# Five answer buffers instead of three, and the landing waits moved from GpSimd to the sync engine, in a mixture-of-experts scatter loop

## What is computed

```python
logits = tokens @ router_w.T
probs = softmax(logits)
rw, re = top_k(probs, 2)                  # each token goes to 2 of 8 experts
rw = rw / rw.sum(-1)
out = tokens
for e in range(8):
    h = gelu(tokens @ w1[e] + b1[e])
    y = h @ w2[e] + b2[e]
    out = out + combine[:, e:e+1] * y     # combine holds rw
```

## Time and profile before

| what | value |
|---|---|
| median of 3 runs | 1566.51 us (1566.21 to 1567.62) |
| the profiled execution's own time | 1572.86 us |
| its span in the trace | 1571.2 us |
| granted TensorE clock, mean over the span | 0.929 |
| second loop, first scatter to last scatter | 892.2 to 1478.3 us |

### The profile page before, as it was taken

The page is one execution under the profiler, slowest core; times in us unless marked ns, Lnnn a source line. Parts: engine busy times, 40 slices in busy tenths (PEclk is TensorE's granted clock), DMA queues, the critical chain, the costliest instruction groups (busy, mean ns, idle before and its releaser), DMA issues. The chain is left out here.

```text
span 1571.2 us, 29272 instructions
## 1 busy us (share of the span) xinstructions
PE 1320.0 (84%) x8768; PEld 1153.5 (73%) x8768; DVE 1018.6 (65%) x3667; ACT 1034.2 (66%) x2256; POOL 919.6 (59%) x932
## 2 busy tenths in 40 slices
PE   2899999999999999999971888888888887887154
PEld 2788888888888888888851777777777777777144
DVE  5488888888887877877856555555555555555022
ACT  2678878878888878888652756666665766665022
POOL 3116556556565665665555167877878787878500
PEclk7999999999999999999975899999999999999567
DMA  8535354354532222321225567777778777776699
GB/s 268 181 115 157 103 165 144 115 166 130 156 108 93 89 99 82 109 99 49 76 82 176 167 117 119 136 128 135 122 128 137 129 135 119 137 128 71 107 408 389
DMA packets 140394, 218.86 MB, mean 139 GB/s; under 512 B 39504, under 2 KB 89936, under 8 KB 139984
## 3 DMA queue, kind: packets, MB, share of 16 engines
q1 hardware_dynamic: 78224, 126.74, 26.4%
q0 software_dynamic: 53184, 71.34, 25.7%
q10 hardware_dynamic: 8832, 18.91, 3.2%
HBM read 103.04 MB, written 118.15 MB: 141 GB/s over the span
## 5 line engine op out<-in xcount | busy, mean ns | idle before, releaser
L1645 POOL DMA_INDIRECT sums<-yy,dest_i x284 | 456.7, 1608 | 162.6 <-issue 68.6
L1509 POOL DMA_INDIRECT sent<-tn,slot_s x256 | 278.3, 1087 | 160.5 <-DVE slot_s L1331 84.6
L1694 PE MATMUL s_bank<-band,hh 128*128 x568 | 175.2, 309 | 91.3 <-DVE yy L1789 91.3
L1789 DVE TENSOR_TENSOR yy<-s_bank,b_all 128x512 f32<-128x512 f32 x142 | 91.5, 686 | 245.4 <-DMA sums<-yy,dest_i 245.2
L1735 ACT ACTIVATE hid<-m_bank,b1s 128x512 f32<-128x512 f32 x142 | 97.4, 688 | 172.5 <-PE m_bank L1677 157.8
L1694 PEld LDWEIGHTS s_bank<-band,hh 128*128 128x128 f32 x568 | 115.6, 204 | 105.4 <-issue 105.3
L1694 PE MATMUL s_bank<-w_s,hh 128*128 x568 | 167.8, 295 | 0.0
L1694 PE MATMUL s_bank<-band,hl 128*128 x568 | 167.7, 295 | 0.0
L1488 POOL TENSOR_TENSOR rs<-ve,halves 128x4 f32<-128x4 f32 x64 | 64.8, 1019 | 151.1 <-DVE ve L1176 151.1
L749 PE MATMUL m_bank<-wvo,band 128*128 128x258 f32 x792 | 133.2, 304 | 13.3 <-DVE band L1317 10.9
L781 PE MATMUL o_bank<-vv,at 128*128 128x256 f32 x512 | 139.8, 396 | 1.3 <-DVE tt L1227 0.7
(11 more groups left out here) (213 smaller groups left out, 3447.6 us busy)
## 6 DMA issues: line engine op xcount, KB each, us to landing
xin<-sent SPq DMA_DIRECT2D x71, 520.0 KB, 4.6
xs<-in_x SPq DMA_DIRECT2D x32, 512.0 KB, 5.0
raw<-in_x SPq DMA_DIRECT2D x32, 512.0 KB
sums<-tt SPq DMA_DIRECT2D x32, 512.0 KB, 3.2
got<-sums SPq DMA_DIRECT2D x32, 512.0 KB, 6.7
out_x<-fin ACTq DMA_DIRECT2D x32, 512.0 KB, 9.0
sums<-yy,dest_i POOLq DMA_INDIRECT x284
raw<-in_x SPq DMA_DIRECT2D x64, 64.0 KB
```

The source lines that it names most:

```text
L1509: eng.indirect_dma_start(sent, bass.IndirectOffsetOnAxis(slot_s[:, par, j, k:k + 1], 0), tn[:, par, k, :], None).then_inc(scattered[par], 16)
L1645: eng.indirect_dma_start(sums, bass.IndirectOffsetOnAxis(dest_i[:, at_ % RING, k:k + 1], 0), yy[:, slot, k, :], None, compute_op=ALU.add). ...
L1694: last = eng.matmul(y_bank[half][:, k * C:(k + 1) * C], hx[:, par, f, ts], rhs, start=(n == 0), stop=(n == 3 * CC - 1))
L1789: eng.tensor_tensor(yy[:, slot, 2 * half:2 * half + 2, :], y_bank[half][:, :].rearrange("p (k c) -> p k c", k=2), b2_all[:, bass.ds(e, 1), ...
```

## The change

The number of `yy` buffers goes from 3 to 5, and with it the number of `rows_out` semaphores and the number of first tiles (n = 1 to 5 in place of 1 to 3) whose wait for tile n-1 is unconditional. The waits for the landings of tiles n-2 and n-1 leave GpSimd. SP takes them in the same round, after its load, and then raises a new semaphore `others_in` by one; GpSimd waits for `others_in` to reach n. What must have landed before a tile's scatters begin stays the same for tiles from 6 on. VectorE waits for the landing of tile n-5 in place of n-3.

```diff
-        YB = 3
+        YB = 5
...
+        others_in = sem("others_in")
...
             @block.sync
...
+                    if it.runs("Z") and it.block("Z") > 0:
+                        at_ = it.block("Z")
+                        if at_ > 1:
+                            eng.wait_ge(rows_out[(at_ - 2) % YB], ((at_ - 2) // YB + 1) * 16 * KT)
+                        if at_ <= YB:
+                            eng.wait_ge(rows_out[(at_ - 1) % YB], 16 * KT)
+                        else:
+                            turn = eng.value_load(turn_i[0:1, at_ - 1:at_], min_val=16 * KT, max_val=16 * KT * TURNS)
+                            eng.wait_ge(rows_out[(at_ - 1) % YB], turn)
+                        eng.sem_inc(others_in, 1)
...
             @block.gpsimd
...
                         if at_ > 0:
-                            if at_ <= YB:
-                                eng.wait_ge(rows_out[(at_ - 1) % YB], 16 * KT)
-                            else:
-                                turn = eng.value_load(turn_i[0:1, at_ - 1:at_], min_val=16 * KT, max_val=16 * KT * TURNS)
-                                eng.wait_ge(rows_out[(at_ - 1) % YB], turn)
-                        if at_ > 1:
-                            eng.wait_ge(rows_out[(at_ - 2) % YB], ((at_ - 2) // YB + 1) * 16 * KT)
+                            eng.wait_ge(others_in, at_)
                         alone(eng, (scaled_d.sem, scaled_d.count(it.before(), "Ys")), (scaled_a.sem, scaled_a.count(it, "Zs")))
```

## The result

The change takes 1557.51 us (median of 4, 1555.85 to 1559.08) against 1567.07 us of the kernel before on the same chip: a ratio of 0.9937 with a 95% interval of 0.992 to 0.9955, or 9.6 us less.

A forecast was written before the change was run, and what follows sets the result against it. GpSimd was taken to bound the loop by its scatters and ten landing waits. Waits falling from 46.8 to 37.2 us took 1566.5 us down 9.6 us to 1557 us, range 1550 to 1569 us.

The forecast's parts named there:

- Parts 1 and 2: Second loop: two more buffers gain 0; tiles 4 and 5 each pay a full landing wait instead of 0.3 us.
- the sum: GpSimd's landing waits in the second loop: 46.8 us before, 37.2 us after, difference -9.6 us.
- Part 3: GpSimd learns of landings through SP and `others_in`: adds 0.1 us per landing wait, bounds 0 and 0.76 us.
- the quiet case: GpSimd's landing wait at the start, with a load issued 4.05 us before the last scatter's end: 2.88 us.
- Part 4: SP's loads, timed by landings, go out 3.8 us before a tile's end; all twelve landing waits become 3.1 us.
- The seven waits: GpSimd's landing waits at expert changes: 34.1 us before, 4.88 us each, predicted to become 3.1 us each.
- the thinnest cover: Front's lead over GpSimd two tiles behind an expert change: 14.9 against 18.3 us, leaving 3.4 us.
- Part 5: VectorE's two line 1777 instructions lengthen GpSimd scatters: 13 us now, taken as unchanged; bounds -13 and +24 us.
- The scatter that lost nothing: GpSimd scatter starting 0.54 us after VectorE's line 1777 work: 1.57 us, read as agreeing only in part with the port rule.
- the costly phase: Timing of VectorE's line 1777 work against scatter starts: claimed narrow; 0.54 us ahead cost nothing, 0.64 us cost 0.52 us.
- the chances: Whole kernel: faster 0.64, from 0.60 less a range tail and 0.03; slower 0.22; same 0.14.

The follow-up runs named there:

- The two load runs: Changed kernel with tiles loaded one round earlier and SP's load before its wait for tile n-1, with three or no further table reads: ratios 1.0072 and 0.9952.

## Why the prediction was right

**What bounds.** GpSimd's scatters and its waits for landings, and not the 245 us on VectorE. The run without first waits shows it most directly: 16 us fewer of GpSimd's waits made the kernel 16 us faster (25.6 against 9.6 us), with no new long wait on GpSimd.

**Parts 1 and 2, the buffers.** Worth 0, and two more first waits. Five against three buffers gave the same ratio once the first waits were gone, and seem to cost 4 us with them (0.9937 against 0.9911, with intervals that overlap); tiles 4 and 5 waited 3.05 and 4.58 us, 7.0 us over their ordinary gaps, where the sum had 5.6 us.

**Part 3, the detour.** The waits over SP came out at 2.98 to 3.14 us where nothing else stretched them, against 2.88 and 3.07 us in the quiet case of before. Counted from the landing's last DMA packet to the next scatter, it is 1.11 to 1.15 us in the kernel before and 1.15 to 1.23 us in the change (without the last expert change). So the hop is near or below the 0.1 us of the sum.

**Part 4, the loads.** This is where the gain came from. The loads fell 3.6 us before a tile's end in the median, where 3.8 us were worked out, and 4.2 us after the end of the tile before; at a change none was in flight. The seven waits fell by 12.3 us (34.1 to 21.8); the sum had 12.4 us. The two load runs on one chip confirm the cause. The front was early enough: every tile from 2 on was weighted 5.8 us or more before its first scatter, where the thinnest cover was worked out as 3.4 us.

**Part 5, the pair.** Taken as unchanged, it gave 3.0 us back in the profiled executions (456.7 to 453.7 us). It was the largest open term and the one that moves most from version to version: 449.1 to 459.5 us over the eleven that kept the pair. Three readings in the prediction do not hold. Not in every case was it the pair: of the 53 scatters over 1.62 us in the kernel before, ten met VectorE's weighting of `yy` (line 1795) and lost up to 0.14 us, that of 1.67 us at 1093.74 us in the earlier trace rows among them. The scatter that lost nothing was no exception, since it began 0.54 us into the instruction, near its end. And the costly phase is not narrow: with a scatter every 1.87 us, a pair costs something wherever one begins in some 1.1 us. By the losses measured above, which fall from 0.55 us to nothing within each of the two instructions, the mean over all phases is an estimated 2 x 0.55 x 0.55 / 2 / 1.87 = 0.16 us a tile, 11 us in 71 tiles, so that a term near its old 13 us was to be expected.

The sum of the waits was -9.6 us; the profiles show 39.3 us in place of 46.8 us, -7.5 us, and the pair's -3.0 us. So the median's -9.6 us agrees with the sum partly by luck, by two small errors of opposite sign. The error in the waits is in two of the first ones, at tile 2 (3.79 us) and tile 5 (4.58 us): I had taken every landing without a load in flight to be quiet. For tile 5 the last load ahead was issued 7 us before tile 4's end and the landing was stretched all the same; the same came back in one other profile (4.46 us in the run without the pair) and not in the runs with the load one round earlier (3.0 to 3.2 us). The trace's DMA packets show what was in flight. Besides the data, they have packets of 16 KB of the kind `instruction`, which the page of the changed kernel lists as one queue:

```profile
q8 instruction: 74, 1.21, 0.3%
```

A landing with no load in flight usually has its last packet 1.8 to 2.0 us after the scatter's end. Over all profiles nine came later, at 2.2 to 3.4 us: that of tile 1 (GpSimd's wait at tile 2) in seven, and that of tile 4 (its wait at tile 5) in the change and in the run without the pair. In all nine such a packet began 0.3 to 0.8 us after the scatter's end, and the landing's last packet came 0.72 to 0.77 us after this one had ended. Four such packets that ended by 1.2 us stretched nothing. So the fetching of the program's own instructions is the likely cause, but no run takes it away, and the prediction had no term for it.

One slip lies in the chances: 0.60 less a tail, plus 0.03, cannot be 0.64.

On the port rule of the Trainium skill ("SBUF — State Buffer", section "Who interferes with whom"): the run without the pair and the rows beside it agree that a VectorE instruction with two SBUF inputs holds up GpSimd's indirect DMAs, and more closely than the prediction's "only in part" had it. A scatter that began inside one waited for what was left of it less 0.13 us. What the rule does not give is the mean, because it hangs on the phase: 9.6 us over 71 tiles, 0.14 us a tile, where the prediction's reading of it had up to 0.64 us.

## What to carry to other kernels

When the engine that waits longest is waiting for another's landings, look at how long finished work lies in front of that other engine: here 7 to 17 us, and more buffers bought nothing. A change that seems to move only waits can retime transfers; ask what each engine issues behind the wait it was given. And where an ordering wait for a landing is on the path, it pays to keep large loads out of its last few microseconds.

## What the runs showed of the hardware

The landing of GpSimd's indirect adding DMA takes longer with a 520 KB load in flight. With a load issued up to 1.5 us before the last scatter's end, GpSimd stood still for 4.5 to 5.3 us at expert changes in four kernels (6.1 us at most, in the run with five further reads). With one issued 2.1 to 2.4 us before it was 3.9 to 4.6 us, with one 2.8 to 3.8 us before 3.0 to 4.4 us, and with none in flight 2.9 to 3.1 us (in most profiles with five buffers 3.5 us at the last change).

A VectorE `tensor_tensor` of 128x512 with both inputs in SBUF lengthens an indirect DMA on GpSimd that begins while it runs, by what is left of the VectorE instruction less 0.13 us, up to 0.52 us. The mean over all 284 starts was 0.03 us. With one input in PSUM it did nothing.

The kernel before took 1567, 1568, 1573 and 1627 us in four sessions. In the slowest, nearly all of the additional time seems to lie ahead of the loop studied here; the kernel before has no trace there, but the version with the load 3.8 us before the end has one in both of the last two sessions. In the slowest its scatters were at:

```profile
L1650 POOL DMA_INDIRECT sums<-yy,dest_i x284: 1557/1562/2082, 947.9 to 1525.0; - x142
```

That is 578.7 us long, as in the other session (578.3 us), but begins 56 us later, of 57 us that the whole span is longer. Its loads of the input at the very start took 8.6 us to land in the median, against 5.0 us. A given saving in us is therefore a smaller share of the time there, by some 4%.
